# Gated cross attention, self attention and experts on one core: the drain of the maxima shared by VectorE and ScalarE

## The chip, the cores and the metric

One core of a Trainium2 chip runs the whole kernel. The metric is the device time of one execution in microseconds, the median of several runs. Engines: PE is TensorE (matmuls), PEld its weight loads, DVE is VectorE, ACT is ScalarE, POOL is GpSimd, SP is the engine that issues most transfers. They run side by side, each its own list in order, and meet at semaphores.

## The reference, cut to what matters

The input is x, 32 items of 112 tokens with 256 features, and for each item a context of 375 rows. Three parts follow each other.

```
x = x + tanh(g0) * cross_attention(layernorm(x), ctx, ctx)      # 16 heads of 16, biases on q, k, v, o
s = layernorm(x)
a = LN(s + self_attention(s))                                   # 16 heads of 16, biases on q, k, v, o
f = sum over the top 2 of 8 experts of gate * (relu(a W1 + b1) W2 + b2)
x = x + tanh(g1) * LN(a + f)
```

Attention is softmax(q k / 4) v. The kernel subtracts each row's maximum before the exponential, so the maxima over all keys are part of the work. The weights of a softmax sum to one, so a bias on v reaches the output as one constant row, bv times Wo, whatever the scores are. The gates of an expert are a softmax over 8 logits; the order of the experts is that of the logits.

## The kernel before

A planner object (`Plan`, `Turn`) lays out the attention as a pipeline over items. One turn takes one step list, `ORDER`, and each letter of a step names a stage that works on its own item: N (first layer norm, item n), A and M (projections and maxima of the cross attention, one item behind), B (its scores and values, two), F (its output and the second norm, three), C (projections of the self attention, four), X and D (its maxima, scores and values, five), E (its output, the gate and the sending to the experts, six). Every engine walks the same list and does its own part of each step, so `ORDER` fixes the order on each engine at once, the queues of SP and GpSimd too. There are 32 full turns, written out without a loop; what is left of the last items after them is sorted by the due times in `LATE`.

PSUM is shared out thus: three banks (`banks`) are handed round among all steps of the pool "bank", each waiting until the use three before it was drained; one tile of four banks, `quad`, serves all steps of the pool "quad" (M.max0 to 3, X.max, B.s0 to 2, D.s), one at a time; `sums` holds the value products of the cross attention. `buffer_free` makes TensorE wait for the last user's drain. Within a turn quad goes through B.s0, X.max, M.max0, B.s1, M.max1, M.max2, D.s, B.s2, M.max3.

Maxima: `maxima` (L1135) makes the scores of a group of heads as queries by keys, row tiles of 32 in the four banks of quad. VectorE's one reduction over all four banks (L896, and L901 for X) writes the row maxima into `row_max`, which has four planes; `M.mT` and `X.mT` turn each plane by a transposition (L1211) and ScalarE copies the 448 columns to `maxT` (L712). `scores` (L1145) then makes keys by queries, with the maxima subtracted by a matmul with -1 (L1151) ahead of the score matmuls (L1154), and ScalarE takes the exponential of all four banks to `probs` (L679). `weigh` (L1158) multiplies by the values.

Other steps that the change touches: A.v drains the values from PSUM on VectorE with the bias added (L879), C.v too (L887); F.out adds the output bias to `proj` (L970), then the residual (L976), then takes the statistics (`measure`, L812); N.ln normalizes x (`normalize`, L827) with the power that GpSimd computes (`invert`, L580), at its place in the order after A.k0; F.oN and E.oN turn the attention's output and VectorE divides it by its sums (`average`, L833); E.gate takes the logits and their maximum, ScalarE their exponential (L738), E.pick the gates, their maximum and the experts' numbers (L918 to L949), E.rank the rows (L950 to L962), E.send two indirect transfers on GpSimd (L624).

After the attention come the experts (63 tiles of 128 rows) and the join, which the change leaves alone. Before they start, SP writes zeros behind each expert's rows once item 30 is ranked (L486), and the last item is sent after that.

## Time and profile before

| | us |
|---|---|
| median of 3 runs (lowest to highest) | 1339.8 (1336.9 to 1344.46) |
| the profiled execution | 1348.36 |
| its span, first to last instruction | 1346.6 |
| PE / PEld busy in the span | 1182.1 / 882.5 |
| DVE / ACT / POOL busy | 849.8 / 573.3 / 244.9 |
| mean granted TensorE clock | 0.967 |

The full turns and the first expert tile share the span so: the first M.mT at 34.62, the last at 957.23, the first matmul of the experts at 1045.92. A matmul's busy time is modelled, and matmuls overlap, so the distance from start to start says more than the duration.

### The profile page before, as it was taken

How to read it: one execution, taken by the hardware profiler on the slowest of the kernel's cores; microseconds unless marked ns; L12 is line 12 of the kernel's file. 1: busy time of each engine (PE TensorE's matmuls, PEld its weight loads, DVE VectorE, ACT ScalarE, POOL GpSimd, SP SyncE). 2: the span in 40 equal slices, each digit the busy share in tenths (PEclk: the TensorE clock that was granted, in tenths of full speed). 3: DMA queues.
4: the chain of work that ended last, by engine and by line, in shares of the span. 5: the costliest groups of instructions: out<-in, count | busy, mean ns of one | idle time of the engine just before them, and what ended most of it. 6: DMA issues, size and time to landing. Idle time of an engine off the chain costs nothing.

```text
span 1346.6 us, 36484 instructions
## 1 busy us (share of the span) xinstructions
PE 1182.1 (88%) x13272; PEld 882.5 (66%) x13273; DVE 849.8 (63%) x2287; ACT 573.3 (43%) x1026; POOL 244.9 (18%) x337
## 2 busy tenths in 40 slices
PE   5788999999998999999999999998873999999964
PEld 2556666666666666666666666666662899999952
DVE  4345566666676666666676666666673466666667
ACT  1334555544545544544555545545541333333300
POOL 1001011211111112111211112111131122222233
PEclk8889999999999999999999999999995899999978
DMA  4122222211111111111111111110012522222255
GB/s 131 58 55 80 71 65 69 68 30 31 30 41 30 31 42 34 34 30 31 31 40 31 30 42 37 30 30 19 9 64 77 174 71 71 70 71 70 62 166 178
DMA packets 60884, 78.52 MB, mean 58 GB/s; under 512 B 12713, under 2 KB 45865, under 8 KB 60617
## 3 DMA queue, kind: packets, MB, share of 16 engines
q1 hardware_dynamic: 46968, 53.58, 14.1%
q0 software_dynamic: 6096, 15.66, 3.5%
q10 hardware_dynamic: 7680, 7.34, 1.7%
q8 instruction: 98, 1.61, 0.5%
q14 instruction: 42, 0.34, 0.1%
HBM read 51.58 MB, written 24.98 MB: 57 GB/s over the span
## 4 chain that ended last, share of the span: by engine, by line
PE 75%; DVE 11%; ACT 5%; issue 4%; DMA 2%; SPq 1%; POOL 0%; DVEq 0%; ACTq 0%; POOLq 0%
PE bank L1132 12%; PE quad L1142 10%; DVE row_max_A L896 9%; PE bank L1291 9%; PE quad L1303 8%; PE quad L1154 8%; PE bank L1194 7%; ACT probs L679 5%; PE bank L1237 4%; PE sums L1165 4%; PE quad L1151 4%; PE bank L1165 2%; PE bank L1229 2%; PE bank L1125 2%; PE bank L1211 1%
## 5 line engine op out<-in xcount | busy, mean ns | idle before, releaser
L679 ACT ACTIVATE probs<-quad 125x1792 f32<-125x1792 f32 (+1 forms) x128 | 213.1, 1665 | 179.1 <-PE quad L1154 179.1
L896 DVE TENSOR_REDUCE row_max_A<-quad 112x4 f32<-112x1500 f32 x128 | 220.1, 1720 | 48.4 <-PE quad L1142 45.5
L624 POOL DMA_INDIRECT sent_dram<-xm,send_row x64 | 61.8, 966 | 432.5 <-DVE send_row L962 389.7
L1142 PE MATMUL quad<-kT_A,qT_A 32*112 32x375 f32 x1024 | 118.1, 531 | 9.2 <-DVE row_max_A L896 5.1
L1291 PE MATMUL bank<-tile_inT,tile_w 128*128 128x128 f32 x1008 | 125.0, 278 | 0.4 <-ACT tile_w L770 0.4
L1291 PEld LDWEIGHTS bank<-tile_inT,tile_w 128*128 128x128 f32 x1008 | 119.6, 195 | 0.8 <-ACT tile_w L770 0.8
L1303 PE MATMUL quad<-output_w,hiddenT 128*128 x504 | 119.1, 380 | 0.0
L1059 DVE TENSOR_SCALAR hiddenT<-bank,hidden_b 128x128 f32<-128x128 f32 x252 | 71.2, 345 | 58.9 <-PE bank L1291 58.7
L1194 PE MATMUL bank<-wxv,ctxT 128*125 128x256 f32 x384 | 103.6, 408 | 0.0
L1132 PE MATMUL bank<-ctxT,wxk 128*128 128x375 f32 x256 | 98.4, 508 | 0.0
L1303 PEld LDWEIGHTS quad<-output_w,hiddenT 128*128 128x128 f32 x504 | 90.9, 190 | 10.0 <-issue 0.2
L1165 PEld LDWEIGHTS sums<-probs,values_A 125*32 125x32 f32 x3072 | 70.9, 110 | 38.9 <-issue 35.3
L641 POOL DMA_INDIRECT kept_dram<-tile_out,take_back x63 | 60.6, 963 | 186.8 <-DVE tile_out L1082 180.3
L1165 PE MATMUL sums<-probs,values_A 125*32 125x112 f32 x3072 | 94.0, 263 | 0.0
L1154 PE MATMUL quad<-qT_A,kT_A 32*125 32x224 f32 x1536 | 90.4, 352 | 0.0
L1194 PEld LDWEIGHTS bank<-wxv,ctxT 128*125 128x125 f32 x384 | 69.4, 194 | 18.1 <-issue 7.3
L1154 PEld LDWEIGHTS quad<-qT_A,kT_A 32*125 32x125 f32 x1536 | 74.2, 186 | 0.2
L901 DVE TENSOR_REDUCE row_max_C<-quad 112x16 f32<-112x1792 f32 x32 | 64.8, 2026 | 7.3 <-PE quad L1142 7.0
L830 DVE TENSOR_SCALAR x_norm<-x_in,moments_N,inv_std_N 112x256 f32<-112x256 f32 x32 | 24.6, 768 | 70.8 <-POOL inv_std_N L589 70.8
L770 ACT ACTIVATE tile_w<-hidden_w 128x1024 f32 x63 | 66.1, 1049 | 0.0
L589 POOL TENSOR_TENSOR inv_std_E<-moments_E,minus_half 112x1 f32<-112x1 f32 x32 | 18.7, 585 | 252.6 <-DVE moments_E L825 251.8
L1142 PEld LDWEIGHTS quad<-kT_A,qT_A 32*112 32x112 f32 x1024 | 37.5, 174 | 38.3 <-ACT probs L679 16.0
(194 smaller groups left out, 1983.2 us busy)
## 6 DMA issues: line engine op xcount, KB each, us to landing
ctxT<-in_ctxT_dram SPq DMA_DIRECT2D x32, 375.0 KB, 3.1
tile_in<-sent_dram SPq DMA_DIRECT2D x63, 129.0 KB
join_in<-kept_dram SPq DMA_DIRECT2D x28, 256.0 KB, 3.4
hidden_w<-in_hidden_w_dram SPq DMA_DIRECT2D x8, 512.0 KB, 4.6
output_w<-in_output_w_dram SPq DMA_DIRECT2D x8, 512.0 KB, 5.3
x_in<-in_x_dram SPq DMA_DIRECT2D x32, 112.0 KB, 2.3
x_res<-in_x_dram SPq DMA_DIRECT2D x32, 112.0 KB, 2.6
kept_dram<-x_shift SPq DMA_DIRECT2D x32, 112.0 KB, 1.9
```

Source lines behind the costliest of these rows:

```text
L679: act.activation(probs[0:rows, t.buffer("probs", step), :, :], quad[0:rows, :, 0:U * T], ACT.Exp, scale=SCALE).then_inc(taken[kind_of(step ...
L770: act.activation(tile_w[:, k, :, :], hidden_w[:, :, bass.ds(e * F, F)], ACT.Copy).then_inc(weights_moved, 1)
L896: dve.tensor_reduce(row_max["A"][:, i, 0:P:ROWS], quad[0:T, :, 0:S], AX_X, ALU.max).then_inc(taken[kind], 1)
L901: dve.tensor_reduce(row_max["C"][:, :, 0:P:ROWS].rearrange("t u r -> t r u"), quad[0:T, :, 0:U * T].rearrange("t r (u s) -> t r u s", s=T) ...
L1059: ins = dve.tensor_scalar(hiddenT[:, k, f, :], hidden_bank[k][:, f * P:(f + 1) * P], hidden_b[:, f, bass.ds(e, 1)], 0.0, ALU.add, ALU.max)
L1132: mm = pe.matmul(out, w[:, c, m * P:(m + 1) * P], actT[:, c, :], start=c == 0, stop=c == DC - 1)
L1142: mm = pe.matmul(quad[0:T, i, at:at + n], qT[a][rows, k, c, e, :], kT[a][rows, k, c, :], start=True, stop=True)
L1154: mm = pe.matmul(quad[0:n, i, c * RH * T:(c + 1) * RH * T], kT[a][rows, k, c, j * n:(j + 1) * n], qT[a][rows, k, c, :, :].rearrange("p e t ...
L1165: mm = pe.matmul(out[h * VW:(h + 1) * VW, g * T:(g + 1) * T], values[a][0:n, k, j, g * G + h, :], probs[0:n, b, i, (c * RH + e) * T:(c * R ...
L1194: mm = pe.matmul(bank[0:SC, (j - first) * D:(j - first + 1) * D], ctxT[:, k, c, j * SC:(j + 1) * SC], wxv[:, c, :], start=c == 0, stop=c = ...
L1291: mm = pe.matmul(hidden_bank[k][:, f * P:(f + 1) * P], tile_w[:, k, c, f * P:(f + 1) * P], tile_inT[:, k, c, :], start=c == 0, stop=c == D ...
L1303: mm = pe.matmul(output_bank[k][:, 0:D], hiddenT[:, k, f, :], output_w[:, f, bass.ds(e * D, D)], start=f == 0, stop=f == FC - 1)
```

## The change

- **Maxima.** VectorE reduces banks 0 and 1 of quad; ScalarE copies banks 2 and 3 as bf16 to `scored_half` in SBUF (two buffers), and VectorE reduces that copy afterwards. TensorE's next use of quad waits for the first reduction and the copy. The maxima of all four heads of a row tile go into one plane of `row_max`, one transposition turns them, and VectorE multiplies the result by a 0/1 column pattern, `place`, into the four column blocks of `maxT`. M.mT and X.mT are drained by VectorE, no longer by ScalarE.
- **Value biases.** A.v is drained by ScalarE as a plain copy, C.v by VectorE as a copy. Once, at the third turn, TensorE multiplies the biases by the output weights (`fold_biases`), and VectorE adds that to the output biases; bxo is multiplied by tanh(g0) as well.
- **Residual.** A new step F.res has GpSimd add the bias to the residual; F.out is one instruction.
- **Gates.** The experts are taken from the logits in E.gate; ScalarE has a second small exponential for the top two; E.pick multiplies it by the inverse sum.
- **Order.** `ORDER` and `LATE` are new.

```diff
-    "A.xT", "A.k0", "N.ln", "B.s0", "A.k1", "F.load", "A.q", "E.oN", "F.oN", "X.max", "N.load", "A.v0", "E.aT",
-    "F.aT", "M.max0", "B.pv0", "C.yT", "E.out", "B.s1", "F.out", "C.bias", "C.qk0", "M.max1", "C.qk1", "B.pv1",
-    "E.norm", "M.max2", "F.shift", "X.mT", "E.xT", "F.norm", "D.s", "E.gate", "C.v", "B.s2", "D.pv", "E.pick",
-    "A.v1", "M.max3", "B.pv2", "E.rank", "E.send", "M.mT"]
+    "N.ln", "A.xT", "A.k0", "B.s0", "F.oN", "A.k1", "A.q", "E.oN", "X.max", "A.v0", "E.aT", "C.yT", "C.bias",
+    "M.max0", "F.aT", "E.out", "X.mT", "N.load", "B.s1", "F.out", "F.load", "F.res", "B.pv0", "M.max1", "E.norm",
+    "C.qk0", "C.qk1", "M.max2", "B.pv1", "E.xT", "D.s", "E.gate", "C.v", "E.pick", "B.s2", "F.norm", "F.shift",
+    "E.send", "A.v1", "D.pv", "M.max3", "B.pv2", "E.rank", "M.mT"]
...
+    "A.k0": 0.59, "A.xT": 0.89, "A.q": 1.04, "A.k1": 1.13, "A.v0": 1.16, "M.max0": 1.20, "M.max1": 1.26,
+    "M.max2": 1.28, "M.max3": 1.54, "A.v1": 1.72, "M.mT": 1.74, "B.s0": 2.00, "B.pv0": 2.26, "B.s1": 2.33,
+    "B.pv1": 2.62, "B.s2": 2.76, "B.pv2": 2.89, "F.oN": 3.08, "F.load": 3.25, "F.aT": 3.30, "F.out": 3.35,
+    "F.res": 3.46, "F.shift": 3.46, "F.norm": 3.59, "C.yT": 3.95, "C.qk0": 4.36, "C.bias": 4.43, "C.qk1": 4.47,
+    "C.v": 4.69, "X.max": 5.14, "X.mT": 5.39, "D.s": 5.66, "D.pv": 5.80, "E.oN": 6.03, "E.aT": 6.21, "E.out": 6.31,
+    "E.norm": 6.51, "E.xT": 6.63, "E.gate": 6.68, "E.pick": 6.75, "E.rank": 6.82, "E.send": 7.09}
...
+     "half": (2, {"M.max", "X.max"})}, LATE, PACE)
...
+        place_of, place = sb("place_of", [P, U, RT]), sb("place", [P, U])
...
+        row_max = {s: sb("row_max_" + s, [T, P]) for s in "AC"}
+        maxT = {s: sb("maxT_" + s, [P, DEEP[s], U, T], BF16) for s in "AC"}
+        scored_half = sb("scored_half", [T, ATTENTION.pools["half"][0], RT // 2 * U * T], BF16)
...
+                if pool == "quad" and kind_of(last[1]) in copied:
+                    eng.wait_ge(copied[kind_of(last[1])], last[0].count(last[1]))
...
+                    elif step == "F.res":
                         k = t.slot("F")
                         if t.base == ATTENTION.lag["F"]:
                             pool.wait_ge(vset, VSET)
-                        pool.wait_ge(resid, t.item("F", 1, 1))
+                        pool.wait_ge(res_loaded[k], t.dmas("F"))
+                        pool.tensor_tensor(x_res[:, k, :], x_res[:, k, :], bxo[0:T, :], ALU.add).then_inc(res_shifted, 1)
+                    elif step == "F.shift":
+                        k = t.slot("F")
+                        pool.wait_ge(taken["F.out"], t.item("F", 1, 1))
                         if t.later("F", 2):
                             pool.wait_ge(x1_stored[k], t.dmas("F", 0))
...
+                    elif kind == "A.v":
+                        if t.base == ATTENTION.lag["A"]:
+                            act.wait_ge(vset, RINGS_SET)
+                        act.wait_ge(made["A.v"], t.count(step))
+                        if t.later("A", DEEP["A"]):
+                            n = ATTENTION.repeats["B.pv"]
+                            act.wait_ge(made["B.pv"], t.item("A", n, (1 - DEEP["A"]) * n))
+                        j, n = ((0, 2), (2, 1))[index_of(step)]
+                        act.activation(values["A"][:, slot_of(t, "A"), j:j + n, :, 0:HD],
+                                       bank[0:SC, 0:n * D].rearrange("s (j h w) -> s j h w", j=n, w=HD),
+                                       ACT.Copy).then_inc(taken["A.v"], 1)
...
-                    elif kind in ("M.mT", "X.mT"):
-                        a = stack_of[s]
-                        scored(act, t, s)
-                        drain(t, step, maxT[a][:, slot_of(t, s), :], bank[:, 0:U * T])
...
-                        act.wait_ge(gate_steps, t.item("E", 9, 2))
+                        act.wait_ge(gate_steps, t.item("E", GATE_STEPS, 3))
                         act.activation(gate_exp[:, :], logits[:, :], ACT.Exp, bias=minus_max[:, :],
                                        accum_out=gate_sum[:, :]).then_inc(gates_exped, 1)
+                        if t.later("E", 1):
+                            act.wait_ge(row_steps, t.item("E", 6, -5))
+                        act.activation(top_exp[:, :], top_logits[:, 0:TOP], ACT.Exp, bias=minus_max[:, :]).then_inc(gates_exped, 1)
+                    elif kind in ("M.max", "X.max"):
+                        act.wait_ge(made[kind], t.count(step))
+                        last = t.before("half", step)
+                        if last is not None:
+                            act.wait_ge(maxed[last[1][0]], last[0].count(last[1]))
+                        n = S if s == "M" else U * T
+                        act.activation(scored_half[:, t.buffer("half", step), 0:RT // 2 * n].rearrange("t (r s) -> t r s", s=n),
+                                       quad[0:T, RT // 2:RT, 0:n], ACT.Copy).then_inc(copied[kind], 1)
                     elif kind == "B.s":
...
+                    for columns, b in ((bxv_columns, bxv), (bsv_columns, bsv)):
+                        dve.tensor_copy(columns[:, :, :], b[:, :].unsqueeze(2).to_broadcast([P, DC, P])).then_inc(columns_set, 1)
+                    dve.wait_ge(folded, 1)
+                    for i, b in enumerate((bxo, bso)):
+                        dve.tensor_tensor(b[:, :], sums[:, i * D:(i + 1) * D], b[:, :], ALU.add).then_inc(biases_set, 1)
+                    dve.wait_ge(biases_set, 2)
+                    dve.tensor_scalar(bxo[:, :], bxo[:, :], tanh_g[:, 0:1], None, ALU.mult).then_inc(vset, 1)
...
+                        dve.tensor_copy(values["C"][:, slot_of(t, "C"), 0, :, 0:HD],
+                                        bank[0:T, 0:D].rearrange("s (h w) -> s h w", w=HD)).then_inc(taken["C.v"], 1)
                     elif kind == "M.max":
                         i = index_of(step)
                         dve.wait_ge(made[kind], t.count(step))
                         if i == 0 and t.later("M", 1):
                             dve.wait_ge(made["M.mT"], t.item("M"))
-                        dve.tensor_reduce(row_max["A"][:, i, 0:P:ROWS], quad[0:T, :, 0:S], AX_X, ALU.max).then_inc(taken[kind], 1)
+                        dve.tensor_reduce(row_max["A"][:, i:P // 2:ROWS], quad[0:T, 0:RT // 2, 0:S], AX_X, ALU.max).then_inc(taken[kind], 1)
+                        dve.wait_ge(copied[kind], t.count(step))
+                        dve.tensor_reduce(row_max["A"][:, P // 2 + i:P:ROWS],
+                                          scored_half[:, t.buffer("half", step), 0:RT // 2 * S].rearrange("t (r s) -> t r s", s=S),
+                                          AX_X, ALU.max).then_inc(maxed[s], 1)
                     elif step == "X.max":
                         dve.wait_ge(made[kind], t.count(step))
                         if t.later("X", 1):
                             dve.wait_ge(made["X.mT"], t.item("X"))
-                        dve.tensor_reduce(row_max["C"][:, :, 0:P:ROWS].rearrange("t u r -> t r u"),
-                                          quad[0:T, :, 0:U * T].rearrange("t r (u s) -> t r u s", s=T),
+                        rows_of = row_max["C"][:, :].rearrange("t (r w) -> t r w", w=ROWS)
+                        dve.tensor_reduce(rows_of[:, 0:RT // 2, 0:U], quad[0:T, 0:RT // 2, 0:U * T].rearrange("t r (u s) -> t r u s", s=T),
                                           AX_X, ALU.max).then_inc(taken[kind], 1)
+                        dve.wait_ge(copied[kind], t.count(step))
+                        dve.tensor_reduce(rows_of[:, RT // 2:RT, 0:U], scored_half[:, t.buffer("half", step), 0:RT // 2 * U * T]
+                                          .rearrange("t (r u s) -> t r u s", u=U, s=T), AX_X, ALU.max).then_inc(maxed[s], 1)
+                    elif kind in ("M.mT", "X.mT"):
+                        a = stack_of[s]
+                        dve.wait_ge(made[kind], t.count(step))
+                        scored(dve, t, s)
+                        dve.tensor_tensor(maxT[a][:, slot_of(t, s), :, :], bank[:, 0:T].unsqueeze(1).to_broadcast([P, U, T]),
+                                          place[:, :].unsqueeze(2).to_broadcast([P, U, T]), ALU.mult).then_inc(taken[kind], 1)
...
+                            dve.wait_ge(gates_exped, t.item("E", 2))
+                            dve.wait_ge(gate_steps, t.item("E", GATE_STEPS))
...
+                        dve.max_index(top_expert[:, :], top_logits[:, :], logits[:, :]).then_inc(gate_steps, 1)
...
-                        dve.wait_ge(gate_steps, t.item("E", 9, 3))
-                        dve.tensor_scalar(gate[:, :], gate_exp[:, :], gate_inv[:, :], None, ALU.mult).then_inc(gate_steps, 1)
-                        dve.wait_ge(gate_steps, t.item("E", 9, 4))
-                        settled(dve, passed_dve)
-                        dve.max(top_gate[:, :], gate[:, :]).then_inc(gate_steps, 1)
-                        dve.wait_ge(gate_steps, t.item("E", 9, 5))
-                        settled(dve, passed_dve)
-                        dve.max_index(top_expert[:, :], top_gate[:, :], gate[:, :]).then_inc(gate_steps, 1)
-                        dve.wait_ge(gate_steps, t.item("E", 9, 6))
...
+                        dve.tensor_copy(top_ids[:, :], top_expert[:, 0:TOP]).then_inc(gate_steps, 1)
+                        dve.wait_ge(gate_steps, t.item("E", GATE_STEPS, 4))
+                        dve.tensor_tensor(chosen[:, :, :], expert_ids[0:T, :].unsqueeze(1).to_broadcast([T, TOP, E]),
+                                          top_ids[:, :].unsqueeze(2).to_broadcast([T, TOP, E]), ALU.is_equal).then_inc(gate_steps, 1)
+                        dve.wait_ge(gate_steps, t.item("E", GATE_STEPS, 5))
                         dve.tensor_tensor(chosen_any[:, :], chosen[:, 0, :], chosen[:, 1, :], ALU.add).then_inc(gate_steps, 1)
+                    elif step == "E.pick":
+
+                        dve.wait_ge(gates_exped, t.item("E", 2, 2))
+                        dve.reciprocal(gate_inv[:, :], gate_sum[:, :]).then_inc(gate_steps, 1)
+                        dve.wait_ge(gate_steps, t.item("E", GATE_STEPS, 7))
 
                         if t.later("E", 2):
                             dve.wait_ge(sent[k], t.dmas("E", 0, TOP))
-                        dve.tensor_scalar(xm[:, k, :, AT_GATE:AT_GATE + 1], top_gate[:, 0:TOP].unsqueeze(2), float(TOP), None,
-                                          ALU.mult).then_inc(row_steps, 1)
+                        dve.tensor_scalar(xm[:, k, :, AT_GATE:AT_GATE + 1], top_exp[:, :].unsqueeze(2), gate_inv[:, :], float(TOP),
+                                          ALU.mult, ALU.mult).then_inc(row_steps, 1)
...
-                        if t.later("F", 1):
-                            dve.wait_ge(resid, t.item("F"))
-                        dve.tensor_tensor(proj[:, :], bank[0:T, 0:D], bxo[0:T, :], ALU.add).then_inc(taken["F.out"], 1)
-                        dve.wait_ge(taken["F.out"], t.count(step))
-                        dve.wait_ge(res_loaded[k], t.dmas("F"))
+                        dve.wait_ge(res_shifted, t.item("F", 1, 1))
                         if t.later("F", 2):
                             dve.wait_ge(normed["F"], t.item("F", 1, -1))
                             dve.wait_ge(shifted, t.item("F", 1, -1))
-                        dve.scalar_tensor_tensor(x1[:, k, :], proj[:, :], tanh_g[0:T, 0:1], x_res[:, k, :],
-                                                 ALU.mult, ALU.add).then_inc(resid, 1)
-                        dve.wait_ge(resid, t.item("F", 1, 1))
+                        dve.scalar_tensor_tensor(x1[:, k, :], bank[0:T, 0:D], tanh_g[0:T, 0:1], x_res[:, k, :],
+                                                 ALU.mult, ALU.add).then_inc(taken["F.out"], 1)
+                        dve.wait_ge(taken["F.out"], t.count(step))
...
+            def fold_biases():
+
+                pe.wait_ge(w_loaded["C"], W_COUNTS["C"] * DMA)
+                pe.wait_ge(columns_set, 2)
+                for i, (w, b) in enumerate(((wxo, bxv_columns), (wso, bsv_columns))):
+                    for c in range(DC):
+                        mm = pe.matmul(sums[:, i * D:(i + 1) * D], b[:, c, :], w[:, c, :], start=c == 0 and i == 0,
+                                       stop=c == DC - 1, skip_group_check=i > 0)
+                mm.then_inc(folded, 1)
+                pe.wait_ge(biases_set, 2)
+
             def turn(t):
                 weights(pe, t, "A", "B", "C")
+                if t.base == ATTENTION.lag["B"]:
+                    fold_biases()
...
-                        for u in range(U):
-                            mm = pe.transpose(bank[:, u * T:(u + 1) * T], row_max[stack_of[s]][:, u, :], ident[0:T, 0:T])
-                        mm.then_inc(made[kind], 1)
+                        pe.wait_ge(maxed[s], t.item(s, n, n))
+                        pe.transpose(bank[:, 0:T], row_max[stack_of[s]][:, :], ident[0:T, 0:T]).then_inc(made[kind], 1)
...
```

## Rows read from the trace of the kernel before

**Rows 1.** Windows view, attention loop: stretch, length, busy us (instructions) per engine, clock.

```profile
504.31:534.44 30.13, 27.79 (x360) 19.62 (x361) 20.23 (x49) 15.20 (x28) 5.03 (x7) 1.00 0.12 34
142.78:926.80 784.02, 722.57 (x9360) 510.28 (x9361) 525.90 (x1245) 395.39 (x728) 129.02 (x180) 1.00 0.13 38
...
926.80:957.23 30.43, 27.59 (x359) 19.58 (x359) 18.96 (x43) 14.66 (x27) 4.67 (x6) 1.00 0.03 9
```

**Rows 2.** Lines view of 142.78 to 926.80: busy, mean ns, idle before with releaser.

```profile
L896 DVE TENSOR_REDUCE row_max_A<-quad 112x4 f32<-112x1500 f32 x104 | 178.8, 1719 | 27.6 <-PE quad L1142 24.7
L679 ACT ACTIVATE probs<-quad 125x1792 f32<-125x1792 f32 x78 | 129.8, 1665 | 92.9 <-PE quad L1154 92.9
...
L901 DVE TENSOR_REDUCE row_max_C<-quad 112x16 f32<-112x1792 f32 x26 | 52.7, 2026 | 6.8 <-PE quad L1142 6.7
...
L1151 PE MATMUL quad<-maxT_A,minus_ones 32*125 32x448 bf16 x312 | 31.8, 398 | 9.2 <-ACT probs L679 9.2
...
L830 DVE TENSOR_SCALAR x_norm<-x_in,moments_N,inv_std_N 112x256 f32<-112x256 f32 x26 | 21.3, 819 | 66.6 <-POOL inv_std_N L589 66.6
...
L1211 PE MATMUL bank<-ident,row_max_A 112*128 112x112 f32 x104 | 14.9, 266 | 22.6 <-DVE row_max_A L896 22.6
...
L666 ACT ACTIVATE maxT_A<-bank 128x448 bf16<-128x448 f32 x26 | 14.1, 544 | 28.4 <-PE bank L1211 28.4
...
L830 DVE TENSOR_SCALAR y<-x,moments_F,inv_std_F 112x256 f32<-112x256 f32 x26 | 10.5, 404 | 0.0
L1151 PE MATMUL quad<-maxT_C,minus_ones 32*112 32x448 bf16 x104 | 10.5, 392 | 29.1 <-DVE row_max_A L896 29.1
```

**Rows 3.** Timeline of one turn: start, duration, engine, line, operation, count, idle before.

```profile
504.31 0.58 PE L1211 MATMUL bank<-ident,row_max_A 112*128 112x112 f32 x4 [0.86 <-DVE row_max_A L896]
...
504.88 0.17 DVE L962 CAST send_row<-route 112x2 uint32<-112x2 f32 x1
...
508.77 0.82 DVE L830 TENSOR_SCALAR x_norm<-x_in,moments_N,inv_std_N 112x256 f32<-112x256 f32 x1 [2.65 <-POOL inv_std_N L589]
...
509.63 0.60 PE L1229 MATMUL bank<-ident,outT_E 128*112 128x128 f32 x4
...
510.75 1.05 PE L1142 MATMUL quad<-kT_C,qT_C 32*112 32x112 f32 x32
510.90 0.25 DVE L840 RECIPROCAL inv_sum_F<-bank 112x16 f32<-112x16 f32 x1
511.18 0.42 DVE L842 TENSOR_TENSOR att_F<-bank,inv_sum_F 112x256 f32<-112x256 f32 x1
...
511.74 1.99 PE L1194 MATMUL bank<-wxv,ctxT 128*125 128x256 f32 x8
...
514.04 0.90 PE L1142 MATMUL quad<-kT_A,qT_A 32*112 32x375 f32 x8
...
514.87 0.97 PE L1165 MATMUL sums<-probs,values_A 125*32 125x112 f32 x32
...
522.85 0.90 PE L1142 MATMUL quad<-kT_A,qT_A 32*112 32x375 f32 x8
...
523.68 0.60 PE L1211 MATMUL bank<-ident,row_max_C 112*128 112x112 f32 x4
...
525.60 0.40 PE L1151 MATMUL quad<-maxT_C,minus_ones 32*112 32x448 bf16 x4 [1.12 <-DVE row_max_A L896]
...
531.61 0.90 PE L1142 MATMUL quad<-kT_A,qT_A 32*112 32x375 f32 x8
...
534.44 0.57 PE L1211 MATMUL bank<-ident,row_max_A 112*128 112x112 f32 x4 [0.86 <-DVE row_max_A L896]
```

**Rows 4.** Waits view, 18 to 142.78, TensorE on VectorE: total, times, longest.

```profile
PE quad L1151 <- DVE row_max_A L896: 8.9, 8, 1.8
...
PE quad L1142 <- DVE row_max_A L896: 5.0, 4, 1.8
```

**Rows 5.** Timeline of the tail: the ranking of item 30 on VectorE.

```profile
1019.96 0.16 DVE L953 TENSOR_TENSOR rows_here<-bank,next_row 112x8 f32<-112x8 f32 x1
```

More of the change, by code:

```diff
@@ L274, in build @@
         gate_inv = sb("gate_inv", [T, 1])
-        gate = sb("gate", [T, E])
-        top_gate = sb("top_gate", [T, 8])
+        top_exp = sb("top_exp", [T, TOP])
+        top_ids = sb("top_ids", [T, TOP])
         top_expert = sb("top_expert", [T, 8], U32)
@@ L321, in build @@
         in_psum = [k for k in ATTENTION.repeats if k.split(".")[1] not in
-                   ("load", "ln", "norm", "pick", "send", "shift", "bias")]
+                   ("load", "ln", "norm", "pick", "send", "shift", "bias", "res")]
         made = {k: sem("made_" + k.replace(".", "_")) for k in in_psum}
@@ L361, in build @@
         vset = sem("vset")
+        copied = {k: sem("copied_" + k.replace(".", "_")) for k in ("M.max", "X.max")}
+        maxed = {s: sem("maxed_" + s) for s in "MX"}
+        columns_set, folded, biases_set = sem("columns_set"), sem("folded"), sem("biases_set")
+        res_shifted = sem("res_shifted")
         rows_zeroed = sem("rows_zeroed")
@@ L597, in turn @@
                         invert(t, "E")
-                    elif step == "F.shift":
+                    elif step == "F.res":
                         k = t.slot("F")
@@ L1150, in scores @@
                 for i, rows in enumerate(tiles):
-                    pe.matmul(quad[0:n, i, 0:U * T], minus_ones[rows, 0:n], maxT[a][rows, k, :], start=True, stop=False)
+                    pe.matmul(quad[0:n, i, 0:U * T], minus_ones[rows, 0:n], maxT[a][rows, k, :, :].rearrange("p u t -> p (u t)"), start=True, stop=False)
                 for c in range(DC):
```

72 lines of the change are left out of this document (24 added, 48 removed).

## The prediction

> **What bounds the kernel now.** I read the page's slices first: TensorE is busy nine tenths or more through most of the span. The windows view then splits the attention loop into turns: 26 equal turns of 784.02 / 26 = 30.15 us, of which TensorE is busy 27.79 in the one I read closely [rows 1]. VectorE has 20.2 and ScalarE 15.2 us in the same turn, so neither is the bound by volume; TensorE, in order, with its waits, is. The lines view names those waits [rows 2]: per turn 29.1 / 26 = 1.12 us before the score matmuls of the self attention (D.s) and 22.6 / 26 = 0.87 before the maxima's transposition (M.mT), both ended by VectorE's reduction, and 9.2 / 26 = 0.35 behind an exponential (B.s2). Together 2.34: 27.79 + 2.34 = 30.13. The reader should see that nine steps a turn share the one four-bank tile quad, and that a step which wants it waits until the drain before it has read all four banks: for maxima 1.72 us of VectorE, for scores 1.67 us of ScalarE.
>
> **Price of the split drain.** VectorE: 1500 elements 1.719, 1792 elements 2.026 [rows 2], so 1.05 ns an element and 0.14 fixed; half is 0.93 (M) or 1.09 (X). ScalarE: 448 elements 0.544, 1792 elements 1.665, so 0.834 ns and 0.17 fixed; half is 0.80 or 0.92. Both start together, so quad is free 0.97 + 0.93 + 0.05 = 1.95 us after M.max starts, where the row shows 2.75 (522.85 to 525.60) [rows 3]. It moves no load off VectorE: it then reduces the copy from SBUF. No row shows a reduction of bf16 in SBUF. Upper end: 0.93 doubled, as x_norm's 0.819 stands to y's 0.404 [rows 2] (the same operation, one beside GpSimd's work, one not); lower end: half the rate, 0.54. I take 0.93, the rate of the rows nearest in kind.
>
> The Trainium skill, "VectorE: DVE Perf Modes", section "The perf-mode tier table", gives tensor_reduce one rate only, whatever the type and memory. By it the value stays 0.93 and the sum as below; with the doubled rate, 0.54, it would be the first rival. No row before has a bf16 reduction, so no trace here shows it yet.
>
> **TensorE's work.** Four transpositions become one, twice a turn. Four last 0.58 [rows 3], one 0.27 (mean 266 ns [rows 2]), so 0.31 each time: 27.79 - 0.62 = 27.17. The multiplication that spreads the result over four columns goes to VectorE: 448 elements, 0.6 us at its rate, where ScalarE had 0.54.
>
> **The waits, walked through the new order**, on TensorE's 35 step starts between 504.31 and 534.44 in the timeline, of which the ones at the waits stand in [rows 3]. A step costs the time from its start to the next one's: M.max 0.83 (514.04 to 514.87), X.max 0.99 (510.75 to 511.74), and read alike F.oN 0.57, E.oN 0.55, scores 1.10, B.pv 0.91 or 0.94, E.out 0.96, F.out 0.95, C.qk0 0.97, C.qk1 1.08. Zero is the start of M.mT.
> - The turn begins with N.ln on VectorE. Its normalization waits for GpSimd, which is still sending: before, send_row was written at 504.88 and x_norm ran 508.77 to 509.59, or +4.46 to +5.28 [rows 3]. All of that comes after VectorE's E.rank, which keeps its place, so the time stays; the 0.6 of the new multiplication and the statistics fit before it. F.oN now goes first on TensorE (at about +2.7) and its drain, 0.70 (510.90 to 511.60 [rows 3]), stands behind x_norm: done at +6.05. E.oN takes the bank of F.oN (three banks in turn), and TensorE arrives at 5.32 (504.31 to 509.63) - 0.31 + 0.57 = 5.58. New wait 0.5; E.oN at 6.1, X.max 6.65, M.max0 at 6.65 + 0.99 + 2.30 (511.74 to 514.04; C.yT stands in for F.aT) = 9.9.
> - From M.max0 (m) to M.max2 TensorE is not held: B.s1 comes 0.83 + 0.28 (F.aT) + 0.96 + 0.12 (X.mT) = 2.19 after M.max0 against 1.95 wanted, M.max1 1.10 + 0.95 + 0.91 = 2.96 after B.s1 against 2.95 (1.23 to fill, 1.67, 0.05), M.max2 at m + 5.15 + 0.83 + 0.97 + 1.08 = 8.03. VectorE's list is: two halves to m + 2.86, E.out and its statistics 1.42 (0.42, 0.43, 0.18, 0.15 and hand-overs), the X.mT multiplication 0.64, F.out 1.48, M.max1's halves, which end at m + 8.35, E.norm 1.0. So M.max2's first half ends m + 10.28, D.s may start m + 10.33, and TensorE is there at 8.03 + 0.83 + 0.94 (B.pv1) + 0.20 (E.xT) = m + 10.0. The old 1.12 leaves 0.3.
> - B.s2 keeps its 0.35: D.s's exponential is as before and E.gate and C.v stand between. M.max3 follows B.s2 by 1.09 + 1.06 (A.v1) + 0.91 (D.pv) = 3.06, B.s2 follows D.s by 2.95. M.mT now waits for both halves: 0.97 + 0.93 + 0.03 + 0.93 + 0.14 = 3.0 after M.max3's start, before 2.83 (531.61 to 534.44). This wait grows to 1.05; only its own shorter work pays.
> Sum: 9.9 + 10.33 + 2.95 + 3.06 + 3.0 = 29.24, so 0.9 less than 30.13. As a check, 27.17 + 0.5 + 0.3 + 0.35 + 1.05 = 29.37. It counts in 27 turns (26 and the like one behind them): 24 us.
>
> **What lies beside.** ScalarE takes 4 x 0.80 + 0.92 for copies, 0.60 + 0.38 for A.v and about 0.3 for top_exp, loses 2 x 0.54: 15.2 + 4.3 = 19.5 of 29.2, hidden; in its order each copy finds it free, but M.max2's, about 0.1 late, still ahead of VectorE. VectorE gives up A.v (0.68 + 0.42), proj (0.42), gate and a second max (0.4) and takes the multiplications (1.2) and five second halves' fixed time (0.7): about even. If that cover were gone, each 0.1 us on a half reduction would cost about 0.4 in a turn (two halves before E.out, two before E.norm, one before M.mT). GpSimd's F.res (0.72, like its other additions) lies in its idle time ahead of F.out; C.bias stands before it, E.norm's power behind it, and nothing waits for either then. F.load moves behind N.load and F.shift on SP's queue; the residual still comes a turn-end early. The folded biases save an addition and cost one stop: at the third turn TensorE waits for two column copies (0.8), four matmuls (1.6) and two additions (0.9) with hand-overs, about 4 us. Ends: 2 if the loads' wait hides half, 8 at TensorE's half clock.
>
> **Beginning and tail.** Up to 142.78 TensorE waits 8.9 + 5.0 = 13.9 us for VectorE at quad, 12 times [rows 4]; 12 x 0.8 = 9.6 and 5 x 0.31 go, minus 4: 7, I take 6 as other waits will move in. The tail (X only, half the waits on normalizations) loses proj and some of the gate chain and ranks item 30 ahead of E.oN of item 31, where its ranking began at 1019.96 [rows 5], which the zeroing of the rows and the last sends follow. I take 4, ends 0 and 8.
>
> **Sum.** 24 + 6 + 4 = 34 us off the profiled 1348.36 (span 1346.6), 1314. That execution is 8.6 above the median shown, 1339.8, so I forecast 1306, ratio 0.975.
>
> **Rivals.**
> - The bf16 half is reduced at double rate (0.54). For: nothing in the rows. Against: all reductions there keep 1.05 ns. D.s's 0.3 and 0.39 of M.mT's wait go: 27 x 0.69 = 19 more, 1287. A like gain comes if GpSimd reaches N.ln's power earlier and E.oN's 0.5 goes: 27 x 0.5 = 13, 1293. Together 0.16.
> - The freed waits come back as others: VectorE, with some 25 us of work and hand-overs in 29, is late at more steps than my walk has. Only the shorter transpositions (0.62) and a third of the waits at the edges are then won: 17 + 3, 1320. For: VectorE stands 2.6 us a turn in N.ln already (66.6 / 26) [rows 2], now at the head of everything. Against: between M.max0 and M.mT its list above fits. 0.16.
> - Slower: SBUF reductions next to GpSimd's work double, to 1.85, as x_norm did. Place: M.max0's and M.max1's second halves, beside F.res, F.shift and the powers. Price: 2 x 0.92 = 1.84 late at D.s, 29.24 + 1.84 = 31.08, 0.95 above the turn of before, so 27 x 0.95 = 26 more than before and 10 less at the edges: 1339.8 + 16 = 1356. It decides once the pair is more than 0.9 + 0.37 (the edges' 10 us over 27 turns) = 1.3 us late. For: 0.819 against 0.404. Against: the reductions from quad keep a mean of 1.719 over 104 [rows 2], GpSimd busy or not, though those read PSUM. 0.06.
> The Trainium skill, "SBUF — State Buffer", section "Who interferes with whom", says a tensor_reduce never contends with GpSimd on this chip while tensor_scalar can. The rows agree as far as they go: x_norm, a tensor_scalar, has the 0.819. By the page the time stays at the forecast; by x_norm's row it is 1356.
>
> **Numbers.** Forecast 0.58, own range 1295 to 1316; larger gain 0.16; freed waits return 0.16; slower 0.06; no change left by mishaps that I have not priced, 0.04. Below 1282 or above 1332 I leave about two in ten of all this. A change under 0.5%, 6.7 us, can't be told from none here. Faster 0.88 (0.58 + 0.16 + all but 0.02 of the third case), same 0.05, slower 0.07.
>
> **What will show it.** M.max halves of 0.93 on VectorE and 0.80 on ScalarE, overlapping; a turn of 29.2; before D.s's first matmul 0.3 instead of 1.12; before M.mT 1.05; a new 0.5 before E.oN's transposition; one stop of 4 us near 36 us. I am wrong if the second half is not near 0.93, if TensorE's idle time per turn stays above 2.3 (the waits came back), or if it falls under 1.7. The experts' part and the join, the last 300 us, should keep their length.

## The result, and the profile after

The changed kernel takes 1297.2 us (median of 6 runs, 1294.49 to 1300.12) against 1339.74 for the kernel before (6 runs beside it on the same chip, 1336.9 to 1344.46): a ratio of 0.968, 95% interval 0.9656 to 0.9703. The forecast was 1306 and faster, with an own range of 1295 to 1316; the time lies near its lower end. The profiled execution took 1300.12 us, its span is 1298.3, 48.3 less than before. The medians differ by 42.5, since the profiled execution of before lay 8.6 above its median and this one lies 2.9 above.

First the page, parts 1 and 5. Columns of part 5: line, engine, operation, count, then busy us, mean ns, idle time before and what ended it.

```profile
PE 1160.2 (89%) x13088; PEld 861.5 (66%) x13089; DVE 824.4 (63%) x2325; ACT 705.4 (54%) x1218; POOL 266.7 (21%) x371
...
L929 DVE TENSOR_REDUCE row_max_A<-quad 112x2 f32<-112x750 f32 x128 | 120.4, 941 | 140.2 <-PE quad L1178 136.1
L774 ACT ACTIVATE scored_half<-quad 112x750 bf16<-112x750 f32 (+1 forms) x160 | 131.9, 824 | 76.4 <-PE quad L1178 73.0
...
L931 DVE TENSOR_REDUCE row_max_A<-scored_half 112x2 f32<-112x750 bf16 x128 | 118.7, 928 | 0.6
```

L929 and L931 answer to the one L896 of [rows 2]: 750 elements from quad in 941 ns, 750 of bf16 from SBUF in 928. The copy kept no reduction waiting: L931 has 0.6 us of such idle time in all.

The windows view: one turn (from D.s to the next D.s), the 26 turns, and what follows up to the experts. Columns as in [rows 1].

```profile
501.29:530.08 28.79, 27.16 (x355) 18.99 (x354) 19.46 (x50) 19.36 (x35) 5.75 (x8) 1.00 0.12 35
...
884.47:909.05 24.58, 23.52 (x269) 16.70 (x269) 16.95 (x40) 16.05 (x30) 5.11 (x7) 1.00 0.07 20
909.05:998.69 89.64, 55.05 (x763) 40.97 (x761) 46.98 (x186) 35.98 (x74) 21.03 (x27) 0.81 0.19 56
135.85:884.47 748.62, 706.00 (x9205) 493.66 (x9205) 504.11 (x1271) 503.34 (x884) 147.53 (x206) 1.00 0.14 40
```

A turn is 28.79 us (748.62 / 26) where it was 30.15 [rows 1], and TensorE's work in it 27.16 where it was 27.79. ScalarE has 19.36 and is still not the bound. The waits view of the same 26 turns says what the rest is, 1.64 us a turn:

```profile
PE bank L1260 <- DVE row_max_A L931: 24.2, 26, 1.1
PE bank L1277 <- DVE att_F L880: 9.4, 25, 0.7
PE quad L1187 <- ACT probs L697: 9.2, 26, 0.4
```

M.mT waits 0.93, E.oN 0.36 (new), B.s2 0.35. The 1.12 before D.s [rows 2] is gone altogether. The timeline around M.max2 and D.s shows why (compare 522.85 to 525.60 in [rows 3]):

```profile
528.01 0.90 PE L1178 MATMUL quad<-kT_A,qT_A 32*112 32x375 f32 x8
...
528.97 0.94 DVE L929 TENSOR_REDUCE row_max_A<-quad 112x2 f32<-112x750 f32 x1
529.08 0.82 ACT L774 ACTIVATE scored_half<-quad 112x750 bf16<-112x750 f32 x1
...
529.94 0.94 DVE L931 TENSOR_REDUCE row_max_A<-scored_half 112x2 f32<-112x750 bf16 x1
530.08 0.13 PEld L1187 LDWEIGHTS quad<-maxT_C,minus_ones 32*112 32x112 bf16 x4
530.08 0.40 PE L1187 MATMUL quad<-maxT_C,minus_ones 32*112 32x448 bf16 x4
```

VectorE and ScalarE empty two banks each at the same time, in 0.94 and 0.82, and TensorE comes at 530.08 to a free tile, with no bracket for a wait.

### The profile page after: what moved, and what is told of

Its sections match the earlier page's. It is cut to its first block, busy times and chain, and to the rows that moved or that the text cites. A ratio compares the mean times of both kernels' runs of the same rounds, so it can differ in the third digit from the quotient of the medians.

```text
span 1298.3 us, 36573 instructions
## 1 busy us (share of the span) xinstructions
PE 1160.2 (89%) x13088; PEld 861.5 (66%) x13089; DVE 824.4 (63%) x2325; ACT 705.4 (54%) x1218; POOL 266.7 (21%) x371
## 4 chain that ended last, share of the span: by engine, by line
PE 68%; DVE 11%; issue 9%; ACT 5%; POOL 4%; DMA 2%; SPq 1%; DVEq 0%; POOLq 0%; ACTq 0%
PE quad L1178 11%; PE bank L1339 9%; PE quad L1351 8%; PE bank L1243 7%; PE bank L1168 6%; PE quad L1190 6%; ACT probs L697 5%; PE bank L1285 4%; PE sums L1201 4%; DVE row_max_A L929 3%; PE quad L1187 3%; POOL sent_dram L642 3%; PE bank L1161 3%; PE bank L1201 2%; DVE row_max_A L931 2%
## 5 line engine op out<-in xcount | busy, mean ns | idle before, releaser
L929 DVE TENSOR_REDUCE row_max_A<-quad 112x2 f32<-112x750 f32 x128 | 120.4, 941 | 140.2 <-PE quad L1178 136.1
L774 ACT ACTIVATE scored_half<-quad 112x750 bf16<-112x750 f32 (+1 forms) x160 | 131.9, 824 | 76.4 <-PE quad L1178 73.0
L931 DVE TENSOR_REDUCE row_max_A<-scored_half 112x2 f32<-112x750 bf16 x128 | 118.7, 928 | 0.6
L1168 PE MATMUL bank<-ctxT,wxk 128*128 128x375 f32 x256 | 95.0, 495 | 0.0
L1190 PE MATMUL quad<-qT_A,kT_A 32*125 32x224 f32 x1536 | 89.3, 349 | 0.0
L1190 PEld LDWEIGHTS quad<-qT_A,kT_A 32*125 32x125 f32 x1536 | 73.5, 184 | 0.1
```

What stands on the lines that cost most here:

```text
L774: act.activation(scored_half[:, t.buffer("half", step), 0:RT // 2 * n].rearrange("t (r s) -> t r s", s=n), quad[0:T, RT // 2:RT, 0:n], ACT ...
L929: dve.tensor_reduce(row_max["A"][:, i:P // 2:ROWS], quad[0:T, 0:RT // 2, 0:S], AX_X, ALU.max).then_inc(taken[kind], 1)
L931: dve.tensor_reduce(row_max["A"][:, P // 2 + i:P:ROWS], scored_half[:, t.buffer("half", step), 0:RT // 2 * S].rearrange("t (r s) -> t r s" ...
L1168: mm = pe.matmul(out, w[:, c, m * P:(m + 1) * P], actT[:, c, :], start=c == 0, stop=c == DC - 1)
L1190: mm = pe.matmul(quad[0:n, i, c * RH * T:(c + 1) * RH * T], kT[a][rows, k, c, j * n:(j + 1) * n], qT[a][rows, k, c, :, :].rearrange("p e t ...
```

## The experiments

All times are medians beside runs of the kernel before on the same chip; the ratio is to those runs. "As after" means the changed kernel with the one edit named. Diffs are cut; "..." marks what is left out.

**Only the split taken back** (one_drain): VectorE reduces all four banks itself, the rest is as after.

```diff
-                        dve.tensor_reduce(row_max["A"][:, i:P // 2:ROWS], quad[0:T, 0:RT // 2, 0:S], AX_X, ALU.max).then_inc(taken[kind], 1)
-                        dve.wait_ge(copied[kind], t.count(step))
-                        dve.tensor_reduce(row_max["A"][:, P // 2 + i:P:ROWS], ...)
+                        dve.tensor_reduce(row_max["A"][:, i:P:ROWS], quad[0:T, :, 0:S], AX_X, ALU.max).then_inc(taken[kind], 1)
...
```

X.max has the same edit, and ScalarE's copies are taken out with their waits.

> The changed kernel with its drain undone: VectorE reduces all four banks in one instruction, ScalarE copies nothing; order, single transposition, folded biases and gates stay. Theory (the split frees the shared tile 0.8 us earlier, and that is worth time where TensorE has too little other work): B.s1 waits 0.56 us again (2.75 wanted, 2.19 there), D.s 0.78 (2.75 against 1.97), B.s2 0.35, M.mT 0.86; a turn of 30.1 instead of 28.79, time 1335. Rival (the new order made the gain, the split nothing): 1297 to 1303.

Measured: 1339.63 us, 0.9996 (0.9974 to 1.0018); the expectation was 5 too low. Its timeline on TensorE shows what the split takes away, a wait before B.s1 and one before D.s:

```profile
506.95 0.65 PE L1259 MATMUL bank<-ident,outT_E 128*112 128x128 f32 x4 [0.35 <-DVE att_F L870]
...
513.56 0.41 PE L1170 MATMUL quad<-maxT_A,minus_ones 32*125 32x448 bf16 x4 [0.54 <-DVE row_max_A L919]
...
522.15 0.40 PE L1170 MATMUL quad<-maxT_C,minus_ones 32*112 32x448 bf16 x4 [0.60 <-DVE row_max_A L919]
...
525.10 0.41 PE L1170 MATMUL quad<-maxT_A,minus_ones 32*125 32x448 bf16 x4 [0.35 <-ACT probs L695]
...
531.00 0.29 PE L1242 MATMUL bank<-ident,row_max_A 112*128 112x112 f32 x1 [0.86 <-DVE row_max_A L919]
```

The turn is 30.00 us (501.00 to 531.00). So without the split the whole rest of the change, shorter transpositions included, gives nothing: in the new order the split is worth 42 us, some 32 of them in the 26 turns (1.21 each). What the gates, F.res and the folded biases give one by one wasn't tried.

**Only the order** (order_alone): the kernel before with the new order and due times (F.res left out, since it has no such step).

> The kernel of before with the new step order and due times, nothing else. Theory: 27.79 of work, B.s1 waits 0.24, D.s 0.78, B.s2 0.35, M.mT 0.87, E.oN 0.16, together 30.2 a turn as before: 1340, ratio 1.00. Rival (the order is the gain): under 1320.

Measured: 1343.05 us, 1.0019 (0.9999 to 1.0039), a turn of 30.02. As expected: by itself the order gains nothing.

**Only the order taken back** (old_order): the split and everything else as after, with the order and due times of before (F.res ahead of M.max0).

```diff
-    "M.max0", "F.aT", "E.out", "X.mT", "N.load", "B.s1", ...
+    "M.max2", "F.shift", "X.mT", "E.xT", "F.norm", "D.s", ...
```

> The changed kernel's code with the step order and due times of before (F.res put ahead of M.max0). Theory: D.s comes only 1.15 us after M.max2 starts and waits 0.80 for the 1.95, the wait before E.oN goes, 27.17 + 0.80 + 0.35 + 0.93 = 29.25 a turn, 27 x 0.46 = 12 more, 1309. Rival (the order is where the gain comes from): above 1330.

Measured: 1425.1 us (1407.5 to 1427.87), 1.060 (1.0543 to 1.0664). This is the great miss of the study: I had 1309. The timeline of one of its turns:

```profile
514.97 1.45 ACT L686 ACTIVATE qT_C<-bank,bsqm,mask 128x112 f32<-128x112 f32 x4 [0.28 <-PE bank L1168]
...
515.77 0.94 DVE L929 TENSOR_REDUCE row_max_A<-quad 112x2 f32<-112x750 f32 x1 [0.26 <-PE quad L1178]
...
516.30 0.81 ACT L774 ACTIVATE scored_half<-quad 112x750 bf16<-112x750 f32 x1
...
517.14 0.94 DVE L931 TENSOR_REDUCE row_max_A<-scored_half 112x2 f32<-112x750 bf16 x1 [0.43 <-ACT scored_half L774]
...
519.75 0.92 DVE L931 TENSOR_REDUCE row_max_A<-scored_half 112x2 f32<-112x750 bf16 x1
520.59 0.61 DVE L948 TENSOR_TENSOR maxT_C<-bank,place 128x448 bf16<-128x448 f32 x1
...
521.35 0.40 PE L1187 MATMUL quad<-maxT_C,minus_ones 32*112 32x448 bf16 x4 [1.84 <-DVE maxT_C L948]
...
521.55 1.55 PE L1190 MATMUL quad<-qT_C,kT_C 32*112 32x224 f32 x16
...
523.80 2.03 PE L1311 MATMUL bank<-wsv,yT 128*112 128x256 f32 x4
...
526.18 1.70 PE L1190 MATMUL quad<-qT_A,kT_A 32*125 32x224 f32 x16
```

Two things are to be read. The copy of M.max1 stands behind ScalarE's drain of qT_C, so the second half waits 0.43 and all behind it on VectorE is late; and X.mT's multiplication, which the change moved to VectorE, is listed behind M.max2's two halves, so D.s waits 1.84 us for it. Then comes what no theory had: after that wait L1190 takes 1.55 instead of 0.92 and L1311 2.03 instead of 1.10, TensorE at its 1.2 GHz level for some 6 us of this turn. By its M.mT starts the turns take 33.5, 33.5 and 31.9 us in rotation (granted clock 0.90 in a long one, 499.53 to 533.02, and 0.95 in a short one, 566.63 to 598.59), 32.96 in the mean of 26 (137.35 to 994.28). The windows view of this kernel:

```profile
400.00:500.00 100.00, 89.97 (x1066) 63.17 (x1067) 59.61 (x152) 58.24 (x103) 17.32 (x24) 0.91 0.11 31
500.00:600.00 100.00, 90.59 (x1067) 63.18 (x1065) 59.54 (x151) 58.46 (x103) 17.33 (x24) 0.91 0.11 31
```

**Where X.mT stands, from both sides.** old_order_turn_early is old_order with X.mT put behind E.out, where the new order has it; turn_late is the changed kernel with X.mT put ahead of E.xT, where the old order had it.

```diff
 old_order_turn_early:
-    "E.out", "B.s1", ..., "F.shift", "X.mT", "E.xT",
+    "E.out", "X.mT", "B.s1", ..., "F.shift", "E.xT",
 turn_late:
-    "E.out", "X.mT", "N.load", "B.s1", ..., "B.pv1", "E.xT",
+    "E.out", "N.load", "B.s1", ..., "B.pv1", "X.mT", "E.xT",
```

> The changed kernel with the order of before, but X.mT behind E.out, where the new order has it. Theory (in the old place VectorE's multiplication for X.mT stands behind M.max2's second half and E.norm, so D.s waited 1.84 us, and TensorE ran at half clock for some 6 us after it in each turn): D.s waits 0.8 to 1.0 again, the clock stays 1.00, a turn of 29.3 to 29.5, time 1309 to 1316. Rival (the rest of the old order is at fault): above 1350 with the clock near 0.91.

> The changed kernel with X.mT alone moved to where the old order had it, in front of E.xT. Theory: the multiplication follows M.max2's second half, D.s starts 3.4 us after M.max2 instead of 2.0, a wait of 1.4, and the clock falls after it as in the old order: a turn of 32 to 33, 1380 to 1410. Rival (a wait of that size costs itself only): 28.79 + 1.4, 1335, clock 1.00.

Measured: 1341.22 us, 0.9994 (0.9975 to 1.0014), and 1342.85 us, 1.0013 (0.999 to 1.0036), ten runs each. The first is 25 us above the 1309 to 1316 of its theory, and its rival, a clock near 0.91, is out too. Both gains end at zero. In the first the granted clock in the turns is 1.00 again, and the turn is 29.87 in the mean (131.09 to 907.79), 3.09 less than old_order's. Its waits are 0.38 before D.s, 0.63 before E.xT, whose E.norm is late behind the 0.43 above, 0.92 before M.mT, 0.35 before B.s2 and, in 20 of the 26 turns, a wait before F.oN that the theory had not, 0.25 in the mean:

```profile
PE bank L1273 <- ACT kT_A L682: 6.6, 20, 0.8
```

Together that is 2.53, where old_order has 1.84 + 0.92 + 0.37 = 3.13. So 0.6 of the 3.09 are waits. The other 2.5 a turn, 65 us over 26 turns, is the half clock: TensorE's busy time for the same instructions falls from 29.82 to 27.31 a turn, in the windows view of old_order and then of old_order_turn_early:

```profile
137.35:994.28 856.93, 775.42 (x9205) 542.89 (x9205) 507.51 (x1271) 503.39 (x884) 148.45 (x206) 0.91 0.12 35
131.09:907.79 776.70, 710.15 (x9205) 497.43 (x9205) 508.16 (x1271) 496.78 (x884) 148.59 (x206) 1.00 0.13 39
```

Against the changed kernel old_order_turn_early reaches the fifth M.mT 4.8 us earlier, loses 1.08 a turn (28 us), and 19 us from the 26th turn's end to the experts (907.8 to 1040.9, 133.1, where it has 114.2). Most of these 19 are the same fault again: the edit moved X.mT in the turns alone, and by the old due times, which order the end, X.mT (5.94) stands just ahead of D.s (6.01). The waits view from 907.79 to 1041 has

```profile
PE quad L1183 <- DVE maxT_C L944: 6.2, 4, 2.6
```

with waits of 2.59, 1.92 and 1.55 us that end at 929.91, 956.42 and 976.42, and behind each the granted clock is 0.50 (929.9 to 936.5, 957.0 to 963.8, 977.4 to 984.0). The changed kernel has no wait for the multiplication there, and a clock of 1.00 from 909.05 to 964. TensorE is busy 89.3 us in that stretch and 78.6 in the changed kernel's, so 10.8 of the 19 are busy time at the lower clock and 6.2 are these waits. In turn_late D.s waits for the multiplication in the turns:

```profile
515.19 0.40 PE L1183 MATMUL quad<-maxT_C,minus_ones 32*112 32x448 bf16 x4 [1.30 <-DVE maxT_C L944]
515.39 0.95 PE L1186 MATMUL quad<-qT_C,kT_C 32*112 32x224 f32 x16
```

1.30 in a turn, and most turns are longer by 1.36 (30.15). In them the clock stays up (0.95 for the 16 matmuls, 0.92 in the changed kernel), so it was mostly the rival that held, a wait that costs itself (1335, 8 us too low); three of the 26 turns take 31.4, with a granted clock of 0.95 in the one from 554.23 to 585.61. One step's place, then, undoes the split's whole gain, and the clock's fall comes on top in one of two orders.

**Four transpositions again** (four_transposes), three of them unused, the rest as after.

```diff
-                        pe.transpose(bank[:, 0:T], row_max[stack_of[s]][:, :], ident[0:T, 0:T]).then_inc(made[kind], 1)
+                        for u in range(U):
+                            mm = pe.transpose(bank[:, u * T:(u + 1) * T], row_max[stack_of[s]][:, :], ident[0:T, 0:T])
+                        mm.then_inc(made[kind], 1)
```

> The changed kernel with the transposition done four times in M.mT and X.mT (three results unused). Theory: X.mT adds 0.31 us a turn in full; M.mT's 0.31 only fills the 0.36 that TensorE waits for VectorE before E.oN, so 27 x 0.31 = 8 us more, 1306, and that wait falls to about 0.05. Rival (every microsecond of TensorE's work counts): 27 x 0.62 = 17, 1314. Second rival (the transpositions stood in waits): 1297.

Measured: 1306.15 us, 0.9745 (0.9726 to 0.9765), 9.0 more than the changed kernel. The wait before E.oN is gone (0.4 us in seven turns), and E.oN starts 5.95 us after M.mT (512.50 to 518.45), as it does in the changed kernel (5.97): what M.mT's shorter transposition gave, that wait took. X.mT's 0.31 counts in 27 turns, 8 us.

**Without the fold** (no_fold): the kernel leaves out what the folded biases add, bv Wo.

> The changed kernel without the folding of the value biases (their contribution bv Wo is left out of the result; neither the column copies nor the four matmuls nor the additions run). Theory: the stop of 6 us at the third turn goes, 1291. Rival (VectorE and the quad chain stand there anyway): 1297.

Measured: 1292.01 us (1289.86 to 1293.46), 0.9631 (0.9605 to 0.9657), 5.2 less than the changed kernel, in whose timeline the stop has 6.10 us (32.85 to 38.95); by the M.mT starts the turn with the stop takes 29.71 there and 23.18 here. The changed kernel's timeline, on TensorE and then VectorE:

```profile
32.85 0.29 PE L1260 MATMUL bank<-ident,row_max_A 112*128 112x112 f32 x1 [2.00 <-DVE row_max_A L931]
34.35 2.04 PE L1212 MATMUL sums<-wxo,bxv_columns 128*128 128x256 f32 x4 [1.21 <-DVE bsv_columns L900]
36.19 1.91 PE L1212 MATMUL sums<-wso,bsv_columns 128*128 128x256 f32 x4
38.95 0.63 PE L1161 MATMUL bank<-ident,x_norm 112*128 112x112 f32 x2 [0.85 <-DVE bso L903]
```

```profile
33.72 0.28 DVE L900 COPY bxv_columns<-bxv 128x256 f32<-128x256 f32 x1
33.92 0.29 DVE L900 COPY bsv_columns<-bsv 128x256 f32<-128x256 f32 x1
38.14 0.42 DVE L903 TENSOR_TENSOR bxo<-sums,bxo 128x256 f32<-128x256 f32 x1 [3.94 <-PE sums L1212]
```

The four matmuls stand as eight in the records, four for each bias, and take 3.75 us at a granted clock of 0.50 (34.35 to 38.10); I had 1.6.

**Towards a better version.** Three edits take on the waits that are left. norm_late puts N.ln behind F.shift; x_norm then doesn't stand ahead of F.oN's drain while GpSimd still sends. values_split gives A.v0 one tile and A.v1 two and puts D.pv behind M.max3, so that TensorE has work while the last maxima are reduced. both_moves has both.

```diff
 norm_late:
-    "N.ln", "A.xT", ..., "F.shift", "E.send", ...
+    "A.xT", ..., "F.shift", "N.ln", "E.send", ...
 values_split:
-    "A.v1", "D.pv", "M.max3", ...
+    "A.v1", "M.max3", "D.pv", ...
...
-                        j, n = ((0, 2), (2, 1))[index_of(step)]
+                        j, n = ((0, 1), (1, 2))[index_of(step)]
```

> The changed kernel with N.ln moved from the head of the turn to behind F.shift, into VectorE's idle 2.4 us before M.max3's reduction, so that neither F.oN stands behind it nor it behind the sends of GpSimd. Theory: the 0.36 before E.oN goes, 27 x 0.36 = 10 less, 1287, and x_norm's wait for GpSimd falls from 2.3 to 0.7. Rival (VectorE has no room there): M.max3's reduction comes late and M.mT's wait grows by as much, 1297 or more.

> The changed kernel with A.v0 making one key tile and A.v1 two (it was two and one) and D.pv moved behind M.max3. Theory: TensorE has 2.89 us of other work between M.max3 and M.mT instead of 1.97, the 0.93 wait goes, M.max3 still finds quad free (2.99 after B.s2 against 2.95) and M.max0 comes 2.40 after X.max against 2.2: 27.86 a turn, 25 less, 1272. Rival (VectorE or ScalarE is the next bound): a new wait at B.s1 or D.s of the same size, 1290 to 1297.

> Both moves, N.ln behind F.shift and the values split 1 and 2 with D.pv behind M.max3. Theory: 28.79 - 0.36 - 0.93 = 27.5 a turn, 35 less than the changed kernel, 1262. Rival (VectorE, busy or handing over 24 of 27.5 us, falls behind): 1275 to 1285, with waits for VectorE at B.s1 or D.s.

Measured: 1284.83 us, 0.9593 (0.9564 to 0.9622); 1279.42 us, 0.9541 (0.9516 to 0.9565); and 1259.84 us (1257.28 to 1263.18), 0.9399 (0.9375 to 0.9424). The three gains are 12, 18 and 37. By the turns they all but add up: 28.22, 28.01 and 27.37 us are 0.57, 0.78 and 1.42 less than 28.79. The rest of the 7 us that the pair gives beyond 12 + 18 lies outside the turns and isn't explained. values_split is 7 above its theory (1272), since 0.15 of M.mT's wait is left in each turn. The waits view of both_moves, 135 to 868:

```profile
PE quad L1183 <- ACT probs L693: 9.2, 26, 0.4
PE bank L1256 <- DVE row_max_A L927: 4.0, 26, 0.2
```

and one turn's length of it (27.37 by its M.mT at 132.25 and 843.77, 26 turns apart):

```profile
500.00:527.50 27.50, 26.99 (x356) 19.16 (x355) 19.18 (x49) 19.55 (x35) 5.69 (x8) 1.00 0.12 36
```

TensorE is busy 98% of the turn. This is the best version found, 80 us below the kernel before.

**The fold spread out** (both_moves_fold_spread): both_moves with the column copies ahead of M.max0's reduction in the first turn that has that step, and one of the fold's four matmuls ahead of each of M.max1, M.max2, M.max3 and M.mT.

> Both moves, and the folding of the value biases spread over the second turn: VectorE makes the columns before M.max0's reduction, TensorE does one of the four matmuls before each of M.max1, M.max2, M.max3 and M.mT, where it waits for VectorE or ScalarE at quad by 1 to 2 us, and waits for the sums only at B.pv0. Theory: the stop of 6 us goes, 1259.8 - 6 = 1254. Rival (the matmuls at half clock lengthen those gaps as much): 1258 to 1260.

Measured: 1263.49 us, 0.9411 (0.9397 to 0.9424), not better than both_moves; the kernel before took 1342.67 beside it and 1339.83 beside both_moves, so the two can't be told apart. On VectorE the copies stand in front of the reductions and wait for the weights:

```profile
23.18 0.29 DVE L911 COPY bxv_columns<-bxv 128x256 f32<-128x256 f32 x1 [7.13 <-DMA gate_w<-in_gate_w_dram]
```

The first M.mT comes at 35.35 instead of 30.65, so most of the stop was traded for a later start: at the fifth M.mT this kernel is 1.3 us ahead (130.91 against 132.25). Whether the fold can be had for nothing from a later turn wasn't tried.

## Why the prediction was right, and where its sizes were off

By the marks M.mT and the experts' first matmul, in us of the two profiled executions:

| stretch | predicted | measured |
|---|---|---|
| start to the fifth M.mT (142.78 before, 135.85 after) | -6 | -6.93 |
| the 26 turns (784.02, 748.62) | -23.4 | -35.40 |
| last turn and tail to the experts (119.12, 114.22) | -4.9 | -4.90 |
| experts and join (300.68, 299.61) | 0 | -1.07 |
| sum | -34 | -48.3 |

Two of these rows fit better than their parts. For the end I had -0.9 for the last turn and -4 behind it; measured are -5.85 (30.43 before, 24.58 after) and +0.95 (88.69, 89.64). The last M.mT already belongs to the steps that `LATE` orders, so this is no turn like the others: the new due times leave less in it (TensorE busy 23.52 for 27.59) and more behind it (55.05 for 52.97). The reasons that I gave for the -4 aren't shown, and that the sum agrees is luck. At the start the fold's turn costs 6.53 (29.71 against 23.18 in no_fold) and not 4, so the freed waits and what else changed there gave some 13.5 where I had 11.2; the two errors nearly cancel.

- **The turn**, the term that was mis-sized: 29.24 predicted, 28.79 measured. By the prediction's own walk: M.mT to E.oN 6.1 against 5.97 (510.19 to 516.16), E.oN to M.max0 3.8 against 3.86, M.max0 to D.s 10.33 against 10.06, D.s to B.s2 2.95 and B.s2 to M.max3 3.06 as predicted, M.max3 to M.mT 3.0 against 2.90. The difference, 0.45, times 26 is the 12 us of the table. The prediction called itself wrong if TensorE's idle time fell under 1.7 us a turn; it is 1.64, since D.s's 0.3 isn't there and M.mT's wait is shorter.
- **D.s's wait**: 0.3 predicted, none measured. I had M.max2's first half end at m + 10.28 because VectorE would be late from M.max1 and E.norm; it ended at m + 9.89 (529.91), 0.39 earlier, since the reduction began as soon as the scores were made, 0.96 after M.max2. M.max2 itself came at m + 7.99 (8.03 predicted).
- **M.mT's wait**: 1.05 predicted, 0.93 measured. The second half starts while the first ends (520.99, 0.94, and then 521.85): the pair takes 1.78 and not 1.89. That it would grow and not shrink was right (0.87 before), and one_drain has 0.86.
- **The new wait before E.oN**: 0.5 predicted and right in size, for the reason given: F.oN's drain (515.40 to 516.09) stands behind x_norm, which waits 2.31 for GpSimd. The view shows 0.36, since it counts from the modelled end of the last matmul; from start to start, as the prediction's walk counts, A.q to E.oN takes 1.40 (514.76 to 516.16), and 0.87 in norm_late (475.69 to 476.56), so the wait costs 0.53. That is also why norm_late gives 0.57 a turn where 0.36 was expected. norm_late takes the wait away by its cause, and four_transposes fills it.
- **TensorE's work**: 27.17 predicted, 27.16 measured. **The copy on ScalarE** 0.80 and 0.92, as predicted; ScalarE 19.5 a turn predicted, 19.36 measured. **The halves** 0.93 and 1.09 predicted; 0.94 and 0.93 for M, 1.09 and 1.07 for X. **The multiplication** 0.6 predicted, 0.62 measured.
- **The reduction of bf16 in SBUF**, the step with no row before: 0.93 taken out of 0.54 to 1.85, 0.928 measured. The Trainium skill, "VectorE: DVE Perf Modes", section "The perf-mode tier table", has one rate for tensor_reduce; the trace now agrees (928 ns of bf16, 941 of fp32 for 750 elements). The rival at 1287 that hung on a double rate is out, and so is the one at 1293, since the wait before E.oN is there.
- **The slower rival** is out by the timeline: GpSimd's x_shift runs 526.62 to 527.35 and the reduction from SBUF starts at 527.03 and takes 0.93, and none of the 128 takes over 0.94. x_norm, which a tensor_scalar computes, takes 0.84 next to y_bias on GpSimd and 0.41 in both_moves, where GpSimd stands idle. The Trainium skill, "SBUF — State Buffer", section "Who interferes with whom", makes just this difference, and the trace agrees.

```profile
514.57 0.72 POOL L631 TENSOR_TENSOR y_bias<-y,bso 112x256 f32<-112x256 f32 x1
514.64 0.84 DVE L868 TENSOR_SCALAR x_norm<-x_in,moments_N,inv_std_N 112x256 f32<-112x256 f32 x1 [2.31 <-POOL inv_std_N L603]
...
526.62 0.73 POOL L623 TENSOR_TENSOR x_shift<-x,ln_shift 112x256 f32<-112x256 f32 x1
...
527.03 0.93 DVE L931 TENSOR_REDUCE row_max_A<-scored_half 112x2 f32<-112x750 bf16 x1
```

- **Freed waits return as others** (0.16): not in this kernel, where TensorE waits 1.64 us a turn, but it is what old_order, old_order_turn_early and turn_late show, which have the split too. The prediction held VectorE's list to be safe; old_order and turn_late show that it is not when X.mT's multiplication stands behind M.max2's halves. I had not priced that place, and my expectation of old_order missed by 116 us, 84 of them for it (1425.1 to 1341.2 in old_order_turn_early).
- **The fold**: 4 us predicted with ends 2 and 8; 6.10 in the timeline, 5.2 by no_fold. The term that failed in it is the matmuls' 1.6. Eight such records, 128x256, take 1.99 at full clock (511.74 in [rows 3]), and the fold's take 3.75 at half.
- **The turn's order as one thing with the drain.** The prediction's sum is right only for both together: neither order_alone (1343), nor the split in the old order (1425), nor the rest without the split (1340) gains anything.
